# A four-layer graph network on one Trainium2 core: more edge columns fetched row by row by SyncE and ScalarE

## The chip, the cores and the metric

One core of one Trainium2 chip runs the whole program. The metric is the device time of one execution in microseconds. The kernel is a single launch; it has no collectives.

## The reference

Four graph layers follow one another on 12500 nodes with 64 features and 412500 edges sorted by `dst`. Each layer normalises the nodes, gathers or sums along the edges, and adds its result to `x`.

```python
h = jnp.maximum(_layernorm(x), 0.0)
m = h[src] * e                                            # layer 0: weighted sum over dst
x = x + segment_sum(m, dst) @ W.T + b
seg_sum, seg_max, cnt = ... of edge_attr by src           # layer 1: pooling of edge features by src
x = x + relu(concat([seg_sum, seg_max, seg_mean, u]) @ W1 + b1) @ W2 + b2
msg = (h @ Wr)[etype, src] / deg[dst]                     # layer 2: relation-wise sum over dst
x = x + ...
a = softmax over dst of leaky_relu(el[src] + er[dst])     # layer 3: attention over dst
x = x + elu(segment_sum(h[src] * a, dst))
```

## The kernel before

The edges are laid out as 128 partitions by 3224 columns, and the columns are cut into 54 chunks of 60 (the last has 44). A "column" is one edge per partition, 128 edges; fetching a column means fetching 128 rows of a table by index. The program is a sequence of blocks, each closed by a barrier of all engines:

1. a first block normalises the nodes and writes `h_table` to HBM;
2. **wsum0**: chunks 0 to 17 of layer 0. GpSimd gathers a column with one indirect DMA (L559), 60 in a row per chunk, into one of two tiles `lead_rows` (`G`). VectorE multiplies by the weights (L723, which frees the tile: `turned`) and scans along the edges (L759); ScalarE copies the scan to `wsum_S` (L892) and stores it (L894). Beside it VectorE and TensorE count the edges per `src` (L603, L604, L951). Chunk 0 is gathered from the raw `x` and normalised in place by VectorE (L688 to L695), with one square root on ScalarE (L842) in the middle. At the end GpSimd gathers chunk 18 ahead (L206);
3. **the sort**: GpSimd first gathers chunk 19 ahead (L206), then scatters the 33-float edge rows to their place by `src`, again one indirect DMA per column (L1079). VectorE, TensorE and ScalarE compute the places; a chunk is handed over at L1153 (`place_ready`). SyncE loads `sort_lows`, `sort_keys` and `sort_feat` for a chunk as soon as the one before it is handed over (L1032 to L1036). After column 15 of a chunk GpSimd waits that the chunk before has landed, and gives its buffer back (`rows_used`, L1086);
4. **the pooled stage**: chunks 18 to 53 of layer 0, gathered as in wsum0, and beside each of them 90 columns of the sorted rows, which SyncE loads into `pool_row` (L537, L538). ScalarE does per chunk, in this order: the index copy for the gathers two chunks on (L867, `index_ready`), the turn of the sorted rows into `pool_Gf` (L847), the copy to `wsum_S` and its store (L892, L894), and two half copies to `pool_S` with a store each (L856, L858), where the second waits for the first store;
5. the updates, and two more gathered stages, **rel** and **att**, each over all 54 chunks.

In rel and att the last two columns of each full chunk are not gathered by GpSimd. SyncE and ScalarE fetch them row by row: `SingleRows.issue` reads 16 byte addresses at a time into registers (L360, a TENSOR_LOAD) and issues 16 DMAs of one row each (L365). Of the 256 rows of a chunk SyncE takes 160 and ScalarE 96 (`BY_SP`). The addresses are computed once, sent to HBM and read back as one row per chunk (`SingleRows.move`, L344 and L347). Rows of chunk k may be issued when its tile is free, that is, when chunk k-2 has been turned; VectorE reads a chunk when GpSimd's columns, SyncE's rows and ScalarE's rows have all landed (`await_rows`). The table `COLUMNS` says how many columns go this way: none in wsum and in the sort, two in rel and att.

Each engine runs its instructions in program order, so a step that stands behind another on its engine waits for it.

## Time and profile before

| | us |
|---|---|
| median of three runs | 16737.31 |
| lowest and highest | 16735.06 and 16739.51 |
| profiled execution, its own time | 16717.65 |
| its span, first to last instruction | 16715.9 |
| wsum0, from the first gather by index to the barrier | 93 to 1436 |
| sort | 1436 to 5616 |
| pooled stage, up to the fetch of the pooled sums | 5616 to 8195 |

GpSimd is busy for 12576.4 us of the span, in its row of 40 slices at 7 tenths nearly everywhere. An indirect DMA is counted busy for about 0.95 us, and about 0.30 us pass before the next one; the profile calls these "issue", time in which the engine waited for nothing that is shown. So 7 tenths is an engine that never stops. VectorE is at 8 or 9 tenths in wsum0 and the sort, 6 or 7 in the pooled stage and 1 or 2 after that. ScalarE is at 2 tenths or less in most slices, though the time it takes to issue DMAs is not in that figure.

### The profile page before, as it was taken

What the parts mean: (1) busy time and instruction counts of PE and PEld (TensorE: products, weight loads), DVE (VectorE), ACT (ScalarE), POOL (GpSimd) and SP (SyncE); (2) the same over time, 40 slices, a digit from 0 to 9 for tenths busy, and PEclk for the clock granted to TensorE, in tenths of its full rate; (3) what the DMA queues carried; (4) which work ended last, traced back from release to release, by engine and by line L of the source; (5) the groups of instructions that cost most, each with busy time, mean ns of one, the idle gap of its engine ahead of it and who ended that gap; (6) DMA issues with size and microseconds to landing.
All of it is one profiled execution on the core that took longest, in us unless ns stands there. A gap on an engine that the chain in (4) does not pass through costs nothing. (4 is left out here: it accounts for less than half of the span.)

```text
span 16715.9 us, 114264 instructions
## 1 busy us (share of the span) xinstructions
PE 2071.2 (12%) x17217; PEld 1933.7 (12%) x17217; DVE 8380.9 (50%) x5953; ACT 2611.6 (16%) x1261; POOL 12576.4 (75%) x13194
## 2 busy tenths in 40 slices
PE   1212333333333111101320000000000000000000
PEld 1212333333323100101210000000000000000000
DVE  7878988888888677777621111111131222222222
ACT  0000111110101232232221111111110110111101
POOL 7777777777777777777767777777777777777776
PEclk9998666666666555555565555555555555555555
DMA  4222211112121233333532222222233222222222
GB/s 80 55 53 68 71 64 63 68 61 70 61 70 61 89 112 114 108 114 108 103 101 56 56 51 56 56 56 51 56 54 41 57 57 52 57 57 57 52 57 56
DMA packets 686784, 1141.43 MB, mean 68 GB/s; under 512 B 407713, under 2 KB 459500, under 8 KB 644044
## 3 DMA queue, kind: packets, MB, share of 16 engines
q0 software_dynamic: 421952, 380.03, 12.4%
q1 hardware_dynamic: 209740, 325.53, 6.6%
q10 hardware_dynamic: 54336, 428.56, 6.4%
q14 instruction: 620, 5.08, 0.1%
q8 instruction: 136, 2.23, 0.1%
HBM read 613.30 MB, written 519.84 MB: 68 GB/s over the span
## 5 line engine op out<-in xcount | busy, mean ns | idle before, releaser
L1079 POOL DMA_INDIRECT by_src<-H,sort_place_i x3224 | 3122.1, 968 | 983.7 <-issue 983.1
L559 POOL DMA_INDIRECT rel_G<-rel_table,rel_idx x3118 | 2945.7, 945 | 984.6 <-issue 951.3
L559 POOL DMA_INDIRECT att_G<-att_table,att_idx x3118 | 2942.2, 944 | 951.3 <-issue 951.3
L559 POOL DMA_INDIRECT lead_rows<-h_table,wsum_idx x3044 | 2887.2, 948 | 927.7 <-issue 927.7
L753 DVE SCALAR_TENSOR_TENSOR rel_Gf<-rel_Sf,rel_keep_first,rel_Gf 128x64 f32<-128x64 f32 x55 | 18.7, 341 | 3386.3 <-ACT rel_Gf L884 3386.3
L727 DVE TENSOR_TENSOR_SCAN att_near<-att_near,er_in 128x60 f32<-128x60 f32 (+2 forms) x55 | 19.3, 351 | 2835.1 <-issue 1846.7
L1247 PE MATMUL pG<-sort_cnt,sort_lowT 128*128 128x98 f32 x6448 | 1116.0, 348 | 816.7 <-DVE sort_prod L1137 816.7
L1247 PEld LDWEIGHTS pG<-sort_cnt,sort_lowT 128*128 128x128 f32 x6448 | 1071.6, 261 | 824.9 <-DVE sort_prod L1137 824.9
L951 PE MATMUL wsum_C<-wsum_high,wsum_low 128*128 128x98 fp8e4 x6448 | 560.9, 282 | 3369.2 <-DVE wsum_high L604 3369.2
L951 PEld LDWEIGHTS wsum_C<-wsum_high,wsum_low 128*128 128x128 fp8e4 x6448 | 520.1, 142 | 3410.6 <-issue 3410.6
L603 DVE TENSOR_TENSOR wsum_low<-iota_b,wsum_parts 128x3840 fp8e4<-128x3840 bf16 x216 | 891.7, 4128 | 9.8 <-DVE wsum_parts L594 9.8
L1129 DVE TENSOR_REDUCE sort_rank<-sort_keys 128x60 f32<-128x7680 int16 (+1 forms) x54 | 784.8, 14533 | 1.8
L884 ACT COPY rel_Gf<-rel_G 128x3840 f32<-128x3840 f32 (+2 forms) x55 | 358.2, 6513 | 2703.6 <-DMA rel_G<-rel_table,rel_idx 2576.2
L1120 DVE TENSOR_TENSOR sort_lowT<-sort_lows,sort_side 128x7680 f32<-128x7680 uint8 (+1 forms) x54 | 704.6, 13048 | 0.0
L1195 ACT COPY sort_cnt<-pC 128x980 f32<-128x980 f32 x323 | 314.7, 974 | 2486.2 <-PE pC L1239 2455.1
L604 DVE TENSOR_TENSOR wsum_high<-iota_b,wsum_parts 128x2940 fp8e4<-128x2940 bf16 x216 | 689.6, 3193 | 0.0
L1137 DVE TENSOR_TENSOR sort_prod<-pG,sort_high 128x980 f32<-128x980 f32 x323 | 374.3, 1172 | 597.7 <-PE pG L1247 597.6
L856 ACT COPY pool_S<-H 128x2880 f32<-128x2880 f32 (+1 forms) x72 | 363.1, 5043 | 1245.1 <-DVE H L636 1054.4
L892 ACT COPY att_S<-att_Sf 128x3840 f32<-128x3840 f32 (+2 forms) x55 | 397.3, 7223 | 907.4 <-DVE att_Sf L759 907.4
L1498 PE MATMUL att_turn<-ident,att_tail 128*66 128x128 f32 x2 | 0.7, 450 | 4169.2 <-DVE att_tail L818 4169.2
L1239 PE MATMUL pC<-sort_high,sort_low 128*128 128x98 bf16 x3224 | 271.0, 250 | 1943.3 <-DVE sort_lowT L1120 1704.9
L1499 PE MATMUL rel_turn<-ident,rel_tail 128*64 128x128 f32 x2 | 0.7, 446 | 3914.8 <-DVE rel_tail L818 3914.8
(368 smaller groups left out, 7624.2 us busy)
## 6 DMA issues: line engine op xcount, KB each, us to landing
rel_G<-rel_table SPq DMA_DIRECT2D x8480, 0.2 KB
att_G<-att_table SPq DMA_DIRECT2D x8480, 0.3 KB
scan_att<-att_S ACTq DMA_DIRECT2D x53, 1980.0 KB
scan_wsum<-wsum_S ACTq DMA_DIRECT2D x53, 1920.0 KB, 6.5
sort_keys<-key_rows SPq DMA_DIRECT2D x53, 1920.0 KB, 9.6
scan_rel<-rel_S ACTq DMA_DIRECT2D x53, 1920.0 KB
scan_pool<-pool_S ACTq DMA_DIRECT2D x70, 1440.0 KB
rel_G<-rel_table ACTq DMA_DIRECT2D x5088, 0.2 KB
```

The lines of the kernel that those rows point to most:

```text
L559: pool.indirect_dma_start(out=G[s][:, j, :], out_offset=None, in_=table, in_offset=bass.IndirectOffsetOnAxis(ap=idx[s][:, j:j + 1], axis=0 ...
L603: v.tensor_tensor(low[b][:, 0:h, :], iota(P), part(0, P), ALU.is_equal, saturate=False)
L604: v.tensor_tensor(high[b][:, 0:h, :], iota(HT), part(1, HT), ALU.is_equal, saturate=False).then_inc(oh_ready, 1)
L856: nc.scalar.copy(pS[:, 0:w // 2, :].rearrange("p j f -> p f j"), run[:, :, rows]).then_inc(ptaken, 1)
L884: nc.scalar.copy(fresh, G[s][:, 0:w, :].rearrange("p j f -> p f j")).then_inc(turned, 1)
L892: nc.scalar.copy(S[s][:, 0:w, 0:D].rearrange("p j f -> p f j"), run).then_inc(taken_out, 1)
L951: last = mm(C[:, way(w)], low[g % NB][:, j, :], high[g % NB][:, j, :], start=False, stop=False, skip_group_check=True)
L1079: pool.indirect_dma_start(out=by_src, out_offset=bass.IndirectOffsetOnAxis(ap=place_i[s][:, j:j + 1], axis=0), in_=row[s][:, j, :], in_off ...
L1120: v.tensor_tensor(lowT[:, 0:n, :], lows[:, 0:P * n].rearrange("p (x j) -> p j x", j=n), own_near.unsqueeze(2).to_broadcast([P, n, P]), ALU ...
L1129: v.tensor_reduce(rank[:, 0:n], keys[:, 0:P * n].rearrange("p (x j) -> p j x", j=n), AX, ALU.add).then_inc(ranked, 1)
L1137: v.tensor_tensor(by_bank(prod[n % 2][:, 0:m, :]), banked(pG[n % 2], 0, m // wide, wide), by_bank(high[:, at:at + m, :]), ALU.mult).then_i ...
L1247: last = mm(pG[n % 2][:, way(w)], lowT[:, WAYS * g + w, :], cnt[n % 2][:, w, :], start=True, stop=True, skip_group_check=True)
```

## The change

The table `COLUMNS` is raised: two columns a chunk go row by row in the two wsum stages, and one in the sort. In wsum the split is that of rel, 160 rows by SyncE and 96 by ScalarE. In the sort all 128 rows go to SyncE. The address table of wsum is made and moved at the start of wsum0, behind the stores of the key rows. In the sort SyncE sends the places of one column to HBM, reads them back as one row, and issues the 128 row stores, after the loads for the next chunk.

The loads of the sorted rows (`pool_row`) move from SyncE to ScalarE, which issues them between its wait for the pooled scan and the first half copy; at the start of the pooled stage ScalarE also takes over the wait for the last scatters.

```diff
-    COLUMNS = dict(wsum=0, sort=0, rel=2, att=2)
-    BY_SP = dict(wsum=0, rel=160, att=160)
+    COLUMNS = dict(wsum=2, sort=1, rel=2, att=2)
+    BY_SP = dict(wsum=160, sort=128, rel=160, att=160)
...
-                        for k in range(1, c1 + 1):
+                        for k in range(1, c1 + 2):
                             rows_of_chunk(k)
                         sp.wait_ge(rows_stored, 96)
                     if pooled:
...
-                        load_rows(0, 0, SIDE)
-                        for k in range(1, NC):
-                            rows_of_chunk(c0 + k + 1)
-                            load_rows(k // 2, k % 2, SHORT if k == NC - 1 else SIDE)
+                        for k in range(2, NC):
+                            rows_of_chunk(c0 + k)
...
                     if raw:
+                        single.await_moved(act)
+                        act_rows_of_chunk(1)
                         act.wait_ge(raw_var_ready, 1)
                         nc.scalar.activation(raw_root[:], raw_var[:], ACT.Sqrt).then_inc(raw_root_ready, 1)
...
+                    def load_rows(k, w=SIDE):
+
+                        act.wait_ge(pscanned, k + 1)
+                        act.dma_start(prow[:, 0:w, :], sorted_rows(0)[:, k * SIDE:k * SIDE + w, :]).then_inc(prow_loaded, 16)
+                        act.dma_start(prow[:, w:w + 1, :], sorted_rows(1)[:, k * SIDE + w - 1:k * SIDE + w, :]).then_inc(prow_loaded, 16)
...
                         act.wait_ge(pscanned, k + 2)
+                        if k + 1 < NC:
+                            load_rows(k + 1, SHORT if k + 1 == NC - 1 else SIDE)
                         for half in range(2):
...
                         own(i, s)
+                        act_rows_of_chunk(c0 + 2 * i + s + 2)
                         if pooled:
                             take_pooled(2 * i + s)
-                        act_rows_of_chunk(c0 + 2 * i + s + 2)
...
+                    if pooled:
+                        await_scattered()
+                        load_rows(0)
...
+                    if counts and not pooled:
+                        act_rows_of_chunk(c1 + 1)
...
-                        sp.dma_start(single_places[s].unsqueeze(1), place_bytes[s][:], allow_slow_non_contiguous=True).then_inc(places_moved, 16)
+                        sp.dma_start(single_places[s].rearrange("(n p) -> p n", p=P), place_bytes[s], allow_slow_non_contiguous=True).then_inc(places_moved, 16)
                         sp.wait_ge(places_moved, 32 * k + 16)
-                        sp.dma_start(place_row[s][:], single_places[s].unsqueeze(0)).then_inc(places_moved, 16)
+                        sp.dma_start(place_row[s], single_places[s].unsqueeze(0)).then_inc(places_moved, 16)
                         sp.wait_ge(places_moved, 32 * k + 32)
...
+                        issue_rows(sp, k, s, sort_by_sp, scattered_sp_rows)
```

GpSimd's part of the program shrinks by these counts: its indirect DMAs of wsum0, of the two chunks ahead, of the sort and of the pooled stage. Before:

```order
L559 DMA lead_rows<-h_table,wsum_idx 128x64 x1020
L206 DMA lead_rows<-h_table,src_all 128x64 x60
L390 UNCONDITIONAL_BRANCH
L1071 UNCONDITIONAL_BRANCH
L1088 IOTA sort_own_part 128x1
L206 DMA lead_rows<-h_table,src_all 128x64 x60
L1079 DMA by_src<-H,sort_place_i 412674x33 x3224
L978 UNCONDITIONAL_BRANCH
L545 UNCONDITIONAL_BRANCH
L559 DMA lead_rows<-h_table,wsum_idx 128x64 x2024
```

and after, with the line numbers of the changed file:

```order
L547 DMA lead_rows<-h_table,wsum_idx 128x64 x986
L209 DMA lead_rows<-h_table,src_all 128x64 x58
L393 UNCONDITIONAL_BRANCH
L1089 UNCONDITIONAL_BRANCH
L1107 IOTA sort_own_part 128x1
L209 DMA lead_rows<-h_table,src_all 128x64 x58
L1097 DMA by_src<-H,sort_place_i 412674x33 x3171
L992 UNCONDITIONAL_BRANCH
L533 UNCONDITIONAL_BRANCH
L547 DMA lead_rows<-h_table,wsum_idx 128x64 x1958
```

Nothing changes place there; 34, 2, 2, 53 and 66 indirect DMAs are gone.

At the start of wsum0 ScalarE has, before, the square root for chunk 0 as its second instruction of the block:

```order
L839 COPY wsum0_idx1<-src_all 128x60
L842 ACTIVATE raw_root<-raw_var 128x60
L867 COPY wsum0_idx0<-src_all 128x60
L892 COPY wsum0_S<-wsum0_Sf 128x64x60
L894 DMA scan_wsum<-wsum0_S 128x3840
```

After, six pairs of a register load and 16 row DMAs stand between; the last two pairs and what follows:

```order
L363 TENSOR_LOAD wsum_single_ids
L368 DMA lead_rows1<-h_table 1x256 x16
L363 TENSOR_LOAD wsum_single_ids
L368 DMA lead_rows1<-h_table 1x256 x16
L838 ACTIVATE raw_root<-raw_var 128x60
L881 COPY wsum0_idx0<-src_all 128x60
L906 COPY wsum0_S<-wsum0_Sf 128x64x60
L908 DMA scan_wsum<-wsum0_S 128x3840
```

The square root has moved behind the rows of chunk 1, and behind the wait for the address table.

In the pooled stage, one chunk of ScalarE after the change, from the last of its six row pairs to the next chunk's store (before, no row pairs and no `pool_row` loads stood on this engine, the rest in the same order):

```order
L363 TENSOR_LOAD wsum_single_ids
L368 DMA lead_rows<-h_table 1x256 x16
L853 DMA pool_row<-by_src 128x2970
L854 DMA pool_row<-by_src 128x33
L870 COPY pool_S<-H 128x64x45
L872 DMA scan_pool<-pool_S 128x2880
L870 COPY pool_S<-H 128x64x45
L872 DMA scan_pool<-pool_S 128x2880
L881 COPY wsum_idx<-src_all 128x60
L859 COPY pool_Gf<-pool_row 128x2880
L906 COPY wsum_S<-wsum_Sf 128x64x60
L908 DMA scan_wsum<-wsum_S 128x3840
```

The index copy for GpSimd stands behind 96 row DMAs, two loads and two half copies.

## Rows read from the trace of the kernel before

**Rows 1.** The page: busy time of each engine.
```profile
PE 2071.2 (12%) x17217; PEld 1933.7 (12%) x17217; DVE 8380.9 (50%) x5953; ACT 2611.6 (16%) x1261; POOL 12576.4 (75%) x13194
```

**Rows 2.** The page, costliest groups: busy and mean, then idle time before.
```profile
L1079 POOL DMA_INDIRECT by_src<-H,sort_place_i x3224 | 3122.1, 968 | 983.7 <-issue 983.1
```

**Rows 3.** GpSimd's indirect DMAs: ns min/median/max, first and last start in us.
```profile
L1079 POOL DMA_INDIRECT by_src<-H,sort_place_i x3224: 965/969/1012, 1527.0 to 5630.4; - x190
L559 POOL DMA_INDIRECT lead_rows<-h_table,wsum_idx x3044: 940/944/4321, 93.0 to 8162.3; - x191
```

**Rows 4.** Row-by-row issue in rel, the same columns; the third is SyncE's waits.
```profile
L365 SPq DMA_DIRECT2D rel_G<-rel_table x8480: 227/228/1132, 8493.3 to 12267.4; - x198
...
L360 SPq TENSOR_LOAD <-rel_single_ids x530: 1135/1255/3667, 8492.0 to 12260.7; - x177
...
SPq L360 <- ACT rel_Gf L884: 102.2, 33, 5.3
```

**Rows 5.** Timeline of ScalarE in rel: start, duration, engine, line.
```profile
8951.17 0.36 ACTq L894 DMA_DIRECT2D scan_rel<-rel_S  x1
8954.59 41.51 ACTq L365 DMA_DIRECT2D rel_G<-rel_table  x96
```

**Rows 6.** Start of wsum0: DMA share and GB/s last; then timelines.
```profile
107.00:114.00 7.00, 0.00 (x0) 0.00 (x0) 6.93 (x3) 0.00 (x0) 6.09 (x4) 1.00 0.14 16
...
121.45 0.25 ACT L842 ACTIVATE raw_root<-raw_var 128x60 f32<-128x60 f32 x1 [69.62 <-DVE raw_var L692]
...
127.38 6.62 DVE L723 TENSOR_TENSOR wsum_Gf<-lead_rows,wsum_near 128x3840 f32<-128x3840 f32 x1
...
178.63 0.24 ACT L867 COPY wsum_idx<-src_all 128x60 int32<-128x60 int32 x1 [28.91 <-DMA lead_rows<-h_table,wsum_idx]
```

**Rows 7.** SyncE: the address table of att sent out and read back.
```profile
L344 SPq DMA_DIRECT2D single_ids_att<-att_single_own x2: 427/5286/10145, 12404.0 to 12404.4; - x2
L347 SPq DMA_DIRECT2D att_single_ids<-single_ids_att x1: 246/246/246, 12448.1 to 12448.1; - x1
```

**Rows 8.** Timeline from wsum0 to the sort, VectorE and GpSimd.
```profile
1302.22 0.22 DVE L721 COPY wsum_near<-wt_all 128x60 f32<-128x60 f32 x1 [14.03 <-DMA lead_rows<-h_table,wsum_idx]
...
1403.71 6.64 DVE L723 TENSOR_TENSOR wsum_Gf<-lead_rows,wsum_near 128x3840 f32<-128x3840 f32 x1
...
1435.87 0.94 POOL L206 DMA_INDIRECT lead_rows<-h_table,src_all  x1 [0.30 <-POOLq L390]
...
1450.75 2.62 DVE L1158 TENSOR_TENSOR H<-H,streams 128x98 f32<-128x98 f32 x9 [14.63 <-POOL sort_own_part L1088]
...
1526.96 1.01 POOL L1079 DMA_INDIRECT by_src<-H,sort_place_i  x1 [1.47 <-issue]
```

**Rows 9.** Sort: SyncE's third load of a chunk; stretch after it (DMA share, GB/s).
```profile
3073.47 0.43 SPq L1036 DMA_DIRECT2D sort_feat<-in_attr  x1
...
3085.00:3089.00 4.00, 0.00 (x0) 0.00 (x0) 4.00 (x2) 0.00 (x0) 2.91 (x3) 0.50 0.06 13
```

**Rows 10.** Timeline of ScalarE in one chunk of the pooled stage.
```profile
7001.13 6.71 ACT L892 COPY wsum_S<-wsum_Sf 128x3840 f32<-128x3840 f32 x1 [10.52 <-DVE wsum_Sf L759]
...
7043.85 0.33 ACTq L858 DMA_DIRECT2D scan_pool<-pool_S  x1
7049.12 5.05 ACT L856 COPY pool_S<-H 128x2880 f32<-128x2880 f32 x1 [5.30 <-DMA scan_pool<-pool_S]
7054.20 0.33 ACTq L858 DMA_DIRECT2D scan_pool<-pool_S  x1
...
7060.14 5.43 ACT L847 COPY pool_Gf<-pool_row 128x2880 f32<-128x2880 f32 x1
```

**Rows 11.** Timeline at the start of the pooled stage, SyncE and ScalarE.
```profile
5632.60 0.32 SPq L537 DMA_DIRECT2D pool_row<-by_src  x1
...
5639.69 5.34 ACT L847 COPY pool_Gf<-pool_row 128x2880 f32<-128x2880 f32 x1 [22.60 <-DMA pool_row<-by_src]
```

**Rows 12.** GpSimd at the end of the pooled stage.
```profile
8194.58 0.94 POOL L1275 DMA_INDIRECT H<-scan_pool,end_src  x1 [31.31 <-DMA scan_pool<-pool_S]
```

More of the change, by code:

```diff
@@ L412, in gathered_layer @@
                 sp_rows = lead["sp_rows"] if counts else [sem(f"sp_rows{q}") for q in range(TURNS)] if by_sp else []
-                act_rows = [sem(f"act_rows{q}") for q in range(TURNS)] if by_act else []
+                act_rows = lead["act_rows"] if counts else [sem(f"act_rows{q}") for q in range(TURNS)] if by_act else []
                 def await_rows(engine, i, s, w=L):
@@ L895, in own @@
                                           S[s][:, 0:w, :]).then_inc(stored[s], 16)
-                    def act_rows_of_chunk(k):
-                        if by_act and k < FULL:
-                            act.wait_ge(turned, k - c0 + 1)
-                            single.issue(act, k, by_act, G[k % 2][:], table, act_rows)
                     def own_and_pooled(i, s):
@@ L1150, in hand_on @@
                         dve.wait_ge(rows_used, k + 2)
-                        if COLUMNS["sort"] and n == L:
-                            v.tensor_scalar(place_bytes[s][:], place[s][:, L - 1:L], rank[:, L - 1:L], float(4 * (A + 1)), ALU.add, ALU.mult)
+                        if n == L:
+                            for m in range(SC):
+                                j = L - SC + m
+                                v.tensor_scalar(place_bytes[s][:, m:m + 1], place[s][:, j:j + 1], rank[:, j:j + 1], float(4 * (A + 1)), ALU.add, ALU.mult)
                         v.tensor_tensor(place_i[s][:, 0:n], place[s][:, 0:n], rank[:, 0:n], ALU.add).then_inc(place_ready, 1)
```

87 lines of the change are left out of this document (49 added, 38 removed).

## The prediction

> **What bounds the kernel now.** I read the page's busy times first. GpSimd is busy for 75% of the span [rows 1], and behind each of its indirect DMAs stands an idle time of "issue" of 0.305 us (983.7 us over 3224), which no other engine ends [rows 2]. So an indirect DMA costs 0.944 + 0.305 = 1.249 us for a gather and 0.969 + 0.305 = 1.273 us for a scatter. The first and last starts agree: the 3224 scatters run from 1527.0 to 5630.4, 1.273 us each with no gap, and the gathers of the pooled stage run on from there to 8162.3 [rows 3]. GpSimd is the bound from the first gather to the end of layer 0, and a column less saves one such price as long as nothing else becomes late. Then I read the timelines of the engines that take the columns over, and asked in each stage what their turn per chunk would be against GpSimd's: 58 x 1.249 = 72.4 us in wsum, 59 x 1.273 = 75.1 us in the sort. All sums are made against the profiled execution (16717.65 us); the median is 19.7 us above it, and I carry the difference over unchanged.
>
> **The gain.** 34 + 2 + 2 + 66 = 104 gathers by 1.249 is 129.9 us, and 53 scatters by 1.273 is 67.5 us: **197.4 us** if GpSimd never waits. Five waits take from it.
>
> **What a row costs.** The same issue is in the trace of rel. SyncE's 53 x 160 rows take 12267.4 - 8493.3 = 3774 us, of which 102 us are waits: 69.3 us a chunk, 0.43 us a row with its share of the register loads [rows 4]. ScalarE's 96 rows take 41.5 us, and the first comes 3.4 us after the store before it was issued [rows 5]. GpSimd kept its pace of 945 ns there, so I charge its gathers nothing for the extra row DMAs. The register loads are 1.255 us for 16 registers [rows 4]. The Trainium skill (Runtime: NRT & Kernel Launch, Instruction fetch mechanics) says that such a load takes about 200 ns a register even in bulk. By that, 16 would be 3.2 us, and the turns below would be longer by some 10 us; the trace disagrees and is used.
>
> **1. Start of wsum0: 38 us.** Before, the square root came at 121.45, chunk 0 was turned 12.6 us later, at 134.0, and GpSimd started chunk 2 at about 177, without a wait [rows 6]. Now ScalarE first waits for the address table. SyncE sends it out behind the key rows, whose transfers end at about 107 (the DMA share falls to 0.14 there) [rows 6]. The same table took 44 us for att, from the issue at 12404.0 to the read-back at 12448.1 [rows 7]; with 3 us for reading back it is there at about 155. Then come 96 rows, 3 + 41.5 us: the square root is at about 200, chunk 0 turned at 212, GpSimd's chunk 2 starts at 213. With two columns less, GpSimd is ready at 175: it waits 38 us. The next chunks have slack (SyncE's rows of chunk 1 end at 155 + 3 + 69 = 227, chunk 3 is gathered from 286 on).
>
> **2. From wsum0 to the sort: 38 us.** SyncE must issue the rows of chunk 19 before the barrier, and may only when chunk 17 is turned. VectorE starts chunk 16 at 1302.2 and, after two counting passes that nothing here shortens, multiplies chunk 17 from 1403.7 to 1410.4 [rows 8]: 108 us later. Plus 69 us of rows and some 2 us of barrier, the barrier opens 179 us after chunk 16's start. GpSimd has work for 72.4 + 72.4 - 1 = 144 us (chunks 17 and 18). Before, the barrier was hidden altogether: it opened at 1435.8 while GpSimd still had 12 gathers queued [rows 8]. Now GpSimd stands still for 35 us. Then the sort's first chunk: before, GpSimd's first scatter came 91 us after the barrier, 15 of which were VectorE's wait for a small GpSimd instruction behind that queue [rows 8]. The rest, 76 to 77 us, stays, against 72.4 us of gathers for chunk 19: 4 us more, less the 1.2 that were idle before. Together 38.
>
> **3. In the sort: nothing.** SyncE's turn is: three loads until 1.6 us after the hand-over, the place column behind them, since the transfers run until about 12 us after it (the DMA share has fallen to 0.06 by 3085; the third load was issued at 3073.5) [rows 9], 2 us each for the way out and back, 3 us to the first row, and 128 x 0.43 = 55 us: about 73 us, below 75.1. It is close, but GpSimd gets a chunk's places some 40 us before it needs them, so SyncE could be over by 0.8 us on each of 50 chunks without a wait. The cover here is VectorE's chunk of about 67 us, which needs the keys only 28 us after the hand-over.
>
> **4. Start of the pooled stage: 10 us.** ScalarE now waits for the last scatters and issues the first `pool_row` load (5632.6 before, by SyncE) ahead of the index copy that GpSimd needs: 3 us. Then its first turn: `pool_Gf` at +7.1 us [rows 11], the rows of chunk 20, and the two half copies stand before the second index copy. That is 68 us after the copy to `wsum_S` starts and comes 7 us after GpSimd is ready for chunk 21.
>
> **5. The turn of ScalarE in the pooled stage: 41 us.** From one copy to `wsum_S` to the next: 6.7 (copy) + 3.4 + 41.5 (rows) + 0.8 (two `pool_row` loads) + 5.1 (half copy) + 5.3 (until the store has landed) + 5.1 (half copy and issue of its store) + 0.5 (index copy) + 5.4 (`pool_Gf`) = **73.8 us** [rows 5, 10]. Before, the same turn had over 40 us of waits in it. Every part waits only for things that are earlier by then, so the turn is ScalarE's own, and since step 4 leaves it behind GpSimd, each of the 32 chunks from 22 on starts when its index copy lets it. With 73.7 (overlaps of a few tenths) that is 32 x (73.7 - 72.4) = 41 us. The bounds: 72.4, where nothing is lost, and 75, 83 us.
>
> **6. Tail of the pooled stage: 21 us.** The last chunks have no rows, but VectorE's pooled scans have been waiting for `pool_Gf`. Before, GpSimd waited 31.3 us for the last `pool_S` store [rows 12]. Following the chain (index copy of chunk 33, scan, load, half copies, `pool_Gf`, scan, 36 us to the next scan, 17 us to the store) I get 108 us from the index copy, against 56 us of gathers left: 52 us of waiting, 21 more.
>
> Sum: 197.4 - 38 - 38 - 10 - 41 - 21 = **49 us gained**, so 16688 us, and about 16669 for a profiled execution. rel and att are not touched.
>
> **The rivals.**
>
> *All is hidden.* GpSimd stays the only bound: 16540 us. For it speaks that rel and att do just this. Against it, in rel ScalarE has far less to do per chunk, and the two ends of wsum0 are serial. 4%.
>
> *ScalarE's turn fits.* If it is 72.4 or less, steps 5 and 6 and most of the 7 us in 4 go: 197.4 - 38 - 38 - 4 = 117 us gained, 16620. Needed is 1.4 us less than summed. 11%.
>
> *Slower: SyncE's turn in the sort.* If the place column takes 5 us each way and the rows 0.45 us each (57.6 us), the turn is 1.6 + 10.4 + 10 + 3 + 57.6 = 83 us. Past a lead of 40 us, GpSimd then waits 51 x (83 - 75.1) - 40 = 363 us, and the kernel is at 17050. It decides from 75.9 us on, and from 76.9 the whole gain is gone: (76.9 - 75.1) x 51 - 40 = 52. 9%, mostly near that point (16700 to 16850).
>
> *ScalarE's turn is longer.* The wait for the `pool_S` store may grow, since the load of `pool_row`, 1.5 MB, is now in ScalarE's own queue just ahead of it, and 160 + 96 rows are under way. At 75.3 us the gain is nil, at 77 us the kernel is slower by 55 us. 10%.
> The skill's 200 ns a register would be the extreme of this: a turn of about 83 us, 32 x 9.5 = 304 us more, 16990. 1%.
>
> *Issue is not the price.* If the 16 DMA engines were the limit, moving issues would change nothing (16737). Their share is 2 to 4 tenths in this part, but for the key stores. 1%. That is where the Trainium skill (DMA: Bandwidth & Descriptors, Issuing engines are not separate DMA queues) points: it says that starting DMAs from several engines saves only sequencer time, usually small beside the transfer. Here that time is the span itself, so the trace does not bear the rule out as an objection. That the change does not do what it says is excluded by the counts of GpSimd's DMAs in the built program.
>
> **How the numbers follow.** The forecast, steps 1 to 6 with a turn of 73 to 74.6 us, has 64%; its own range is 16660 to 16720 (turn 20 to 70 us lost, start and boundary +-8 each). The range reaches down to the case where the turn fits and up to the first part of the slower ones: 16620 to 16750. About 0.2% (33 us) is what a measurement of this kernel can tell from no change, so faster is below 16704. Of the 64%, 50 lie there and 14 above; with 4 and 11 from the first rivals faster has 65%. Same gets those 14, 5 of the longer turn, 2 of the sort and the 1 of the DMA engines: 22%. Slower has 13%.
>
> **What would show it.** In the profile after: the square root at about 200 instead of 121; GpSimd idle for 35 us at its first gather of the sort's block, waiting for SyncE through the barrier; scatters again 1.273 us apart with no wait; GpSimd waiting for ScalarE's index copy some 30 times, 1 to 2 us each, and copies to `wsum_S` 73 to 74.5 us apart; the last wait of the stage at 52 us. If the scatters show waits for the place computation (`place_ready`), step 3 is wrong; if the pooled chunks stand 72.4 us apart, step 5 is; if the square root is before 165, step 1 is. A different pace of GpSimd's gathers beside rows (not 0.944 us) would make all of it wrong.

## The result and the profile after

| | before | after |
|---|---|---|
| median of 4 runs | 16736.62 us (16735.06 to 16739.51) | 17565.91 us (17564.64 to 17570.26) |
| span of the profiled execution | 16715.9 us | 17568.4 us |

The changed kernel is slower by 829 us: 1.0496 times the kernel before, 95% interval 1.0478 to 1.0514. 16688 was forecast, in a range up to 16750.

The loss is in one stage. GpSimd's indirect DMAs by line (count, ns min/median/max, first and last start), to be held against [rows 3]:

```profile
L1097 POOL DMA_INDIRECT by_src<-H,sort_place_i x3171: 964/970/1009, 1553.6 to 6433.5; - x199
...
L547 POOL DMA_INDIRECT lead_rows<-h_table,wsum_idx x2944: 939/945/4546, 93.2 to 8985.8; - x197
```

A scatter takes 970 ns as before, and there are 53 fewer. Yet they run for 4880 us instead of 4103. At the old pace 3171 of them take 4037 us; 843 us are waiting. The pooled stage, from there to the last gather, takes 2552 us (2532 before). From the list of waits of GpSimd (us in total, times, longest us):

```profile
POOL lead_rows L547 <- ACT wsum_idx L881: 99.5, 33, 7.0
POOL H L1300 <- DMA scan_pool<-pool_S: 51.7, 1, 51.7
POOL lead_rows L547 <- DVE wsum_Gf L711: 36.3, 1, 36.3
POOL sort_own_part L1107 <- POOLq L393: 36.1, 1, 36.1
```

These are steps 4 and 5, step 6, step 1 and step 2 of the forecast. (The 33 waits of the first line hold 0.3 us each that pass before every gather, 10 us in all.) The waits of the sort are not under a name: the page puts them under "issue", and has 1807.6 us of idle time ahead of 3171 scatters, where 0.305 each would be 967:

```profile
L1097 POOL DMA_INDIRECT by_src<-H,sort_place_i x3171 | 3076.0, 970 | 1807.6 <-issue 1799.0
```

What GpSimd waits for is seen on SyncE. One chunk of the sort in its timeline (start, duration, line, what it issues); compare [rows 9]:

```profile
3477.30 0.36 SPq L1062 DMA_DIRECT2D sort_lows<-low_rows  x1
3477.72 0.42 SPq L1063 DMA_DIRECT2D sort_keys<-key_rows  x1
3478.19 0.42 SPq L1066 DMA_DIRECT2D sort_feat<-in_attr  x1
3478.71 0.47 SPq L1072 DMA_DIRECT2D single_places<-H  x1
3495.55 0.24 SPq L1074 DMA_DIRECT2D H<-single_places  x1
3501.47 66.96 SPq L1046 DMA_DIRECT2D by_src<-H  x128
3568.55 0.36 SPq L1062 DMA_DIRECT2D sort_lows<-low_rows  x1
```

SyncE goes round in 91.25 us here, 91.4 in the mean of its turns, and after the first hand-over it waits for no other engine in the sort, only for its own DMAs. GpSimd needs 75.1. At its column 15 GpSimd waits until SyncE's rows of the chunk before have landed, 13.9 us here:

```profile
3478.81 0.97 POOL L1097 DMA_INDIRECT by_src<-H,sort_place_i  x1 [13.92 <-issue]
```

Step 3 had about 73 us for this turn. Of its terms, the rows are off most: 66.96 us for 128, where 55 were forecast. The row DMAs themselves are alike in both places (227 ns, [rows 4]). What differs is the register load ahead of every 16 of them:

```profile
L1041 SPq TENSOR_LOAD <-H x424: 3432/3542/3757, 1574.0 to 6388.7; - x142
...
L363 SPq TENSOR_LOAD <-rel_single_ids x530: 1132/1253/4916, 9334.4 to 13107.0; - x177
...
L363 SPq TENSOR_LOAD <-wsum_single_ids x520: 1136/1255/4673, 154.1 to 8881.0; - x174
```

The median is 3.54 us instead of 1.25, for 16 registers each. Eight of them a chunk make 8 x 2.3 = 18.3 us, and 91.25 - 18.3 = 73.0. So the question for the experiments is why the same instruction costs 2.8 times as much in the sort.

The change put the places into the spare part of `H`. In the built program `H` begins at byte 52448 of its partition, the spare part 19760 bytes further on, and `place_row` 2 words behind that: 72216, which is 8 bytes behind a multiple of 16. The batches of ids begin at multiples of 32 (117408 for rel, 121920 for wsum, 104832 for att, each plus multiples of 64). Theory A is the address. Theory B is something else about the place: the tile was just written by a DMA, or lies in partition 0, or the stage has heavy vector work and 3.8 MB of loads a chunk.

### The profile page after: what moved, and what is told of

It is laid out like the page before. It is cut to its first block and busy times, and to the rows that moved or that the text cites. A ratio compares the mean times of both kernels' runs of the same rounds, so it can differ in the third digit from the quotient of the medians.

```text
span 17568.4 us, 155834 instructions
## 1 busy us (share of the span) xinstructions
PE 1942.9 (11%) x17217; PEld 1813.1 (10%) x17217; DVE 8384.2 (48%) x6008; ACT 2604.8 (15%) x1261; POOL 12454.3 (71%) x13037
## 5 line engine op out<-in xcount | busy, mean ns | idle before, releaser
L1097 POOL DMA_INDIRECT by_src<-H,sort_place_i x3171 | 3076.0, 970 | 1807.6 <-issue 1799.0
L547 POOL DMA_INDIRECT lead_rows<-h_table,wsum_idx x2944 | 2804.6, 953 | 1023.8 <-issue 887.1
L1272 PE MATMUL pG<-sort_cnt,sort_lowT 128*128 128x98 f32 x6448 | 1019.7, 328 | 819.8 <-DVE sort_prod L1156 819.8
L1272 PEld LDWEIGHTS pG<-sort_cnt,sort_lowT 128*128 128x128 f32 x6448 | 975.3, 241 | 827.9 <-DVE sort_prod L1156 827.9
L1264 PEld LDWEIGHTS pC<-sort_high,sort_low 128*128 128x128 bf16 x3224 | 222.9, 116 | 2890.4 <-DVE sort_lowT L1139 2889.3
```

Source lines behind the costliest of these rows:

```text
L547: pool.indirect_dma_start(out=G[s][:, j, :], out_offset=None, in_=table, in_offset=bass.IndirectOffsetOnAxis(ap=idx[s][:, j:j + 1], axis=0 ...
L1097: pool.indirect_dma_start(out=by_src, out_offset=bass.IndirectOffsetOnAxis(ap=place_i[s][:, j:j + 1], axis=0), in_=row[s][:, j, :], in_off ...
L1264: last = mm(pC[:, way(w)], low[:, WAYS * g + w, :], high[:, WAYS * g + w, :], start=False, stop=False, skip_group_check=True)
L1272: last = mm(pG[n % 2][:, way(w)], lowT[:, WAYS * g + w, :], cnt[n % 2][:, w, :], start=True, stop=True, skip_group_check=True)
```

## The experiments

Seven of the fifteen fell on chips where every kernel is much slower, the kernel before too (24142 to 24227 us instead of 16716 to 16737); the section on the hardware has what is different there. Below, these are called slow chips and the others good chips. From the slow chips only durations of single instructions are used, and ratios where it is said. Five of the seven were repeated on a good chip or have a counterpart there; e2_shifted_ids and e14_places_at_16 have not, so what they would cost or gain in time is not known. In the experiments on good chips the kernel before takes 16715 to 16718 us. A ratio is always against the kernel before on the same chip.

### The places at another address (e1_aligned, e5_aligned_again, e7_aligned)

```
-place_row = [spare[0:1, 2 * SC + s * SC * P:2 * SC + (s + 1) * SC * P] for s in range(2)]
+place_row = [spare[0:1, 12 + s * SC * P:12 + (s + 1) * SC * P] for s in range(2)]
```

> The changed kernel with one number changed: `place_row` begins 12 words into the spare part of `H` instead of 2, so that each batch of 16 places that SyncE loads into registers begins at a multiple of 64 bytes of the partition, as the batches of `wsum_single_ids` do (now it begins 24 bytes behind a multiple of 32). Same tile, same partition, same freshness, same stage. Theory A, the address makes the register load slow: the loads of line 1041 fall from 3.43 to 3.76 us to 1.25 us, SyncE's turn from 91.3 us by 8 x 2.3 = 18 us to about 73, GpSimd's scatters stand 1.273 us apart again (75.1 us a chunk), and the kernel is at 17566 - 52 x (91.3 - 75.1) = about 16725 us. Theory B, the load is slow because the tile was just written by a DMA, or because of its partition or the stage: the loads stay at 3.4 to 3.8 us and the time at 17566 us.

> The same kernel as e1_aligned (the changed kernel with `place_row` moved to a multiple of 64 bytes), for a chip on which the kernel before takes 16737 us: where e1_aligned ran, it took 24142 us, since there SyncE and ScalarE often started only one instruction in 1.4 us in the long lists of row DMAs. That run has shown that the loads of the places now take 1.23 us; what it could not show is what this is worth. Theory A: 16725 us, SyncE's turn in the sort about 73 us, scatters 1.273 us apart. If the place column's wait of 16.8 us (16 us behind the loads of the chunk) or anything else in the turn keeps SyncE above 75.1 us, it shows as 52 times the excess.

> The changed kernel with `place_row` at a multiple of 64 bytes, once more, now for the time where the kernel before takes about 16730 us. Theory A (the slow loads are what pushed SyncE's turn over GpSimd's): loads 1.23 us, a turn of about 73 us, scatters 1.273 us apart, 16725 us. If something else in the turn keeps it above 75.1 us, such as the 16.8 us in which the place column goes out behind the loads, the loads are fast and the kernel still stands above that, at 16725 + 52 times the excess.

In e1_aligned (27261 us beside 24142) and e5_aligned_again (27407 beside 24227) the loads took 1.23 us, but the time said nothing on the question. e7_aligned: **16714.17 us beside 16717.61, ratio 0.9999 (0.9989 to 1.0008)**. Moving one tile by 40 bytes takes back all of the 5%. The loads, the scatters, and SyncE's chunk:

```profile
L1041 SPq TENSOR_LOAD <-H x424: 1132/1231/1452, 1572.7 to 5466.3; - x142
```

```profile
L1097 POOL DMA_INDIRECT by_src<-H,sort_place_i x3171: 965/969/1011, 1551.3 to 5588.0; - x199
```

```profile
3454.39 0.36 SPq L1062 DMA_DIRECT2D sort_lows<-low_rows  x1
...
3455.80 0.65 SPq L1072 DMA_DIRECT2D single_places<-H  x1
3472.57 0.24 SPq L1074 DMA_DIRECT2D H<-single_places  x1
3475.76 51.21 SPq L1046 DMA_DIRECT2D by_src<-H  x128
3527.09 0.36 SPq L1062 DMA_DIRECT2D sort_lows<-low_rows  x1
```

This turn is 72.7 us, and the scatters take 4036.7 us, 1.273 each. Tile, partition, stage and freshness are the same, so theory B is out. SyncE's first 28 turns of the sort are 73.2 us each in the mean; after that they are 75.1 us apart, since SyncE has caught up with the hand-over and waits for it.

### The same shift in another stage (e2_shifted_ids)

```
-self.ids = sb(f"{kind}_single_ids", [FULL, self.columns * P], I32, c)
+self.step = BATCH + 1 if kind == "rel" else BATCH
+self.ids = sb(f"{kind}_single_ids", [FULL, self.columns * P // BATCH * self.step], I32, c)
...
-engine.load(registers, self.ids[k:k + 1, r0:r0 + BATCH])
+at = r0 // BATCH * self.step
+engine.load(registers, self.ids[k:k + 1, at:at + BATCH])
```

> The kernel before, with nothing changed but the spacing of the ids of rel in SBUF: a batch of 16 every 17 words instead of every 16, so that the ten loads of SyncE begin 0, 4, 8, 12, 16, 20, 24, 28, 0, 4 bytes behind a multiple of 32 and the six of ScalarE 8, 12, 16, 20, 24, 28. The ids of att keep their spacing, as a control. Theory A: the load costs 1.25 us where it begins at a multiple of 32 bytes and about 3.5 us at 24 behind one, where it does so in the sort of the changed kernel; how it goes between is what this run shows. If all but the multiples of 32 are slow, SyncE's turn in rel is 69.3 + 8 x 2.3 = 88 us against GpSimd's 72.4 and rel is longer by up to 52 x 15 = 800 us (about 17530 us); if multiples of 8 or 16 were fast too it would be less. Theory B: all sixteen loads stay at 1.25 us, since these ids lie long in place, and the time is 16737 us.

24697 us beside 24142, one run on a slow chip, so only the loads count (count, ns min/median/max; att is the control):

```profile
L363 SPq TENSOR_LOAD <-rel_single_ids x530: 275/3526/3907, 10298.1 to 17506.2; - x177
L363 SPq TENSOR_LOAD <-att_single_ids x530: 3/1242/1471, 17865.7 to 24487.6; - x177
```

Batch by batch, medians of the 53 loads of each in us, by the bytes at which the batch begins behind a multiple of 32:

| engine | 0 | 4 | 8 | 12 | 16 | 20 | 24 | 28 |
|---|---|---|---|---|---|---|---|---|
| SyncE | 1.25, 1.26 | 3.63, 3.63 | 3.54 | 1.59 | 0.70 | 3.63 | 3.63 | 3.63 |
| ScalarE | - | - | 7.30 | 0.88 | 1.32 | 3.77 | 3.77 | 3.78 |

Column 12 and SyncE's 16 are disturbed by that chip: the batches of att in the same places of the row are disturbed too (0.70 to 0.80 us). ScalarE's 8 is its first load of each turn, which is slow on good chips too: 3.10 us in att here, and 2.99 and 3.06 us in rel and att of the kernel before on a good chip, all at multiples of 32. That is a second cause of slow loads, and what it is was not asked. What is left is plain: fast at 0 and 16, slow at 4, 8, 20, 24 and 28; 12 stays open.

### Is the step 16 or 32 bytes (e14_places_at_16)

```
-place_row = [spare[0:1, 2 * SC + s * SC * P:2 * SC + (s + 1) * SC * P] for s in range(2)]
+place_row = [spare[0:1, 8 + s * SC * P:8 + (s + 1) * SC * P] for s in range(2)]
```

> The changed kernel with `place_row` 24 bytes further on, at a multiple of 16 bytes that is none of 32. By e2_shifted_ids (ScalarE's batch 16 bytes behind a multiple of 32 took 1.32 us, those 4, 8, 12, 20, 24 and 28 behind mostly 3.5 to 3.8) the step is 16 bytes: loads of 1.23 us and 16714 us, as e7_aligned. Rival, the step is 32 bytes: loads of 3.5 us and about 17560 us, as the changed kernel.

This ran on a slow chip (27395 us beside 24210), but the loads answer:

```profile
L1041 SPq TENSOR_LOAD <-H x424: 2/1228/1425, 2682.9 to 8599.7; - x142
```

The load takes 1.23 us at an address that is a multiple of 16 and not of 32, so a multiple of 16 bytes is enough. The expected 16714 us could not be tested there. Its ratio to the kernel before (1.1315) is that of e5_aligned_again (1.1318), but the kernel with slow loads was not run on such a chip.

### The turn is a sum (e12_places_first)

The slow loads stay, and SyncE sends the place column out and back ahead of the chunk's three loads:

```
 sp.sem_inc(loading, 1)
+if k:
+    send_places(k - 1, 1 - s)      # place_bytes -> single_places -> place_row
 sp.dma_start(lows[:].unsqueeze(1), ...)
```

> The changed kernel with its slow register loads (`place_row` as it is, 8 bytes behind a multiple of 16), but SyncE sends the place column out and back ahead of the three loads of a chunk instead of behind them. This takes the other large part, the wait of 16.8 us, out of SyncE's turn: 91.3 - 16.8 + 2.1 for the way out on free queues = 76.6 us, or 74.5 if the way back is hidden as well by the issues of the loads. Theory (the turn is a sum, and what counts is by how much it exceeds 75.1): 0 to 1.5 us over on each of 52 chunks, 16714 (as e7_aligned) to 16792 us, with the slow loads still at 3.5 us. Rival: the register load is slow in itself and the wait was only filled by it, or the delayed loads of the chunk (2 to 3 us) make VectorE late: above 16850 us.

**17130.48 us beside 16717.57, ratio 1.0247 (1.0232 to 1.0263)**: 338 us above my theory's upper end, and where the rival had put it (above 16850 us). SyncE's chunk shows which number was wrong:

```profile
3467.12 0.36 SPq L1072 DMA_DIRECT2D single_places<-H  x1
3475.56 0.23 SPq L1074 DMA_DIRECT2D H<-single_places  x1
3475.85 0.34 SPq L1064 DMA_DIRECT2D sort_lows<-low_rows  x1
...
3482.02 67.83 SPq L1046 DMA_DIRECT2D by_src<-H  x128
3549.98 0.36 SPq L1072 DMA_DIRECT2D single_places<-H  x1
```

The way out takes 8.4 us with nothing ahead of it, not 2.1; it is 128 transfers of 4 bytes, one a partition. So of the 16.8 us in the changed kernel only half was waiting behind the loads. I had taken this term from the wrong row (the way back, one row of 512 bytes).

Of the rival's two causes, one is out: the loads stay at 3.55 us although the other wait in the turn has halved. The other was that VectorE gets its loads late and is late itself. GpSimd's waits do bear that name now, 402.7 us of them:

```profile
POOL by_src L1103 <- DVE sort_place_i L1180: 402.7, 48, 10.2
```

But VectorE stands idle for 14 us a chunk until its loads come, and SyncE, which issues them, waits for VectorE only once, before the first chunk. The pace is SyncE's turn, 83.1 us in the mean (the one shown has 82.9). The scatters take 4439.3 us, 403 more than 4037. With the rule that is derived below, 53 turns by (83.1 - 75.1) less a cover of 20 us make 404. The turn is a sum, and each us over 75.1 costs 53.

### Each part alone (e3_sort_alone, e9_sort_alone, e4_wsum_alone, e10_wsum_alone)

The kernel before has tiles of their own for the places, at multiples of 64 bytes, so e3 and e9 have fast loads. The edits of e4 and e10 also leave out the place tiles and SyncE's part in the sort.

```
-COLUMNS = dict(wsum=0, sort=0, rel=2, att=2)      # of the kernel before
+COLUMNS = dict(wsum=0, sort=1, rel=2, att=2)      # e3, e9
```

```
-COLUMNS = dict(wsum=2, sort=1, rel=2, att=2)      # of the changed kernel
+COLUMNS = dict(wsum=2, sort=0, rel=2, att=2)      # e4, e10
```

> The kernel before, with the one scattered column a chunk by SyncE in the sort alone (none in wsum), and the places in tiles of their own, whose addresses are multiples of 64. Theory A: SyncE's turn is about 73 us, below GpSimd's 75.1, so each of 53 scatters of 1.273 us is gained: 16737 - 67 = 16670 us, and the register loads take 1.25 us. A rival, that the sort's stage itself (its heavy vector work, 3.8 MB of loads a chunk, 2 queues) makes SyncE slow: a turn near 91 us and about 17510 us.

> The kernel before with the column a chunk by SyncE in the sort alone, the places in tiles of their own at multiples of 64 bytes, once more for the time where the kernel before takes about 16730 us: 53 scatters of 1.273 us less, 67 us below the kernel before.

> The changed kernel without SyncE's scatters in the sort (the place columns are not sent either; all 60 columns by GpSimd): the part of the change in wsum alone, with ScalarE loading the sorted rows. From the two traces: the first scatter is 26.6 us later than before (1553.65 against 1527.0), the sort takes its 4103 us as before, and the pooled stage from the last scatter to the last gather is 2552 against 2532 us: 16737 + 27 + 20 = 16784 us. If instead the pooled stage was slowed by something that the slow sort left behind, it is nearer to the 49 - 67 = 18 us of loss that my forecast gives this part: 16755 us.

> The changed kernel without SyncE's scatters in the sort, once more for the time where the kernel before takes about 16730 us: the first scatter 27 us later and the pooled stage 20 us longer than before, so 47 us above the kernel before. With e9_sort_alone it should add up to e7_aligned: 47 - 67 = 20 us below the kernel before.

Slow chip: e3_sort_alone 24923 us and e4_wsum_alone 26458 us beside 24142. Good chip: **e9_sort_alone 16650.79 us beside 16717.61, ratio 0.9961 (0.9946 to 0.9975)**, 67 us gained, as the 53 scatters had promised. **e10_wsum_alone 16784.18 us, ratio 1.0039 (1.0025 to 1.0053)**, 67 us lost, where I had expected 47: my sum had left out the last wait of GpSimd, which grew by 20 us (51.5 instead of 31.3, [rows 12]). Together they cancel, and e7_aligned, which has both, is within 4 us of the kernel before. So the wsum part of the change was a loss by itself: 104 gathers are worth 130 us, and its waits cost that and 67 more. GpSimd's two largest waits in e10_wsum_alone:

```profile
POOL lead_rows L547 <- ACT wsum_idx L881: 103.7, 34, 7.3
POOL H L1301 <- DMA scan_pool<-pool_S: 51.5, 1, 51.5
```

### ScalarE's wait filled (e8_pool_batch_between)

ScalarE's turn in the pooled stage of the changed kernel, from one copy to `wsum_S` to the next (compare [rows 10]):

```profile
7506.15 6.73 ACT L906 COPY wsum_S<-wsum_Sf 128x3840 f32<-128x3840 f32 x1
...
7515.99 40.72 ACTq L368 DMA_DIRECT2D lead_rows<-h_table  x96
...
7557.78 5.09 ACT L870 COPY pool_S<-H 128x2880 f32<-128x2880 f32 x1 [44.90 <-issue]
...
7569.89 5.05 ACT L870 COPY pool_S<-H 128x2880 f32<-128x2880 f32 x1 [7.02 <-DMA scan_pool<-pool_S]
...
7575.34 0.24 ACT L881 COPY wsum_idx<-src_all 128x60 int32<-128x60 int32 x1 [0.40 <-ACT pool_S L870]
7575.49 5.30 ACT L859 COPY pool_Gf<-pool_row 128x2880 f32<-128x2880 f32 x1
7580.68 6.75 ACT L906 COPY wsum_S<-wsum_Sf 128x3840 f32<-128x3840 f32 x1
```

```
 act.dma_start(scan_pool..., pS[:, 0:w // 2, :]).then_inc(pstored, 16)
+if half == 0 and k < NC - 2:
+    act_rows_of_chunk(c0 + k + 2, -BATCH)      # the last 16 rows, between the half copies
```

> As e7_aligned, and in the pooled stage ScalarE issues the last 16 of its 96 rows of a chunk between the two half copies, where it waited 7.0 us for the `pool_S` store. Theory: ScalarE's turn (75.4 us) is what bounds the pooled stage; it falls to about 68.5, GpSimd's 72.4 is the bound again, 32 x 3.0 = 96 us are won on e7_aligned: about 16630 us. Rival, that the 75.4 us come from elsewhere (the gathers themselves are slower beside the rows, or VectorE is the bound): nothing changes against e7_aligned.

**16645.87 us beside 16717.61, ratio 0.9957 (0.994 to 0.9974)**, 68 us below e7_aligned on the same chip, where 96 were expected. In its list of waits the 104.2 us for ScalarE's index copy have become 7.1, so ScalarE's turn did bound the stage. Of these 97 us, 9 are no gain: they are the 0.3 us that pass before any gather. The last wait grew by 13 (52.0 in e7_aligned), the pooled scans of VectorE and ScalarE ending that much later behind the gathers.

```profile
POOL H L1302 <- DMA scan_pool<-pool_S: 65.1, 1, 65.1
...
POOL lead_rows L547 <- ACT wsum_idx L883: 7.1, 4, 3.3
```

The rest is small: the wait at the start is 39.8 us here and 36.3 in e7_aligned, and the 2944 gathers are busy for 2800.6 us instead of 2796.6. That makes 97 - 9 - 13 - 4 - 4 = 67.

### The start and the boundary (e6_all_mended, e11_start_mended, e13_keys_by_scalar, e15_keys_by_scalar_again)

e6_all_mended is e8_pool_batch_between with the ids sent out first, the square root ahead of ScalarE's first rows, and the rows of chunk 19 issued in the sort (SyncE's at its first chunk, ScalarE's 96 in six batches, one in each of six chunks):

```
+single.move(sp)                                   # ahead of the key stores
 sp.wait_ge(rows_made, 1)
...
-single.await_moved(act)
-act_rows_of_chunk(1)
 act.wait_ge(raw_var_ready, 1)
 nc.scalar.activation(raw_root[:], raw_var[:], ACT.Sqrt).then_inc(raw_root_ready, 1)
+single.await_moved(act)
+act_rows_of_chunk(1)
...
 load_chunk(k, k % 2)                              # SyncE in the sort
+if k == 0:
+    lead_single.issue(sp, lead_chunk, range(0, BY_SP["wsum"]), lead["rows"][1][:], h_table, lead["sp_rows"])
```

> The changed kernel with four edits, each against one of the losses read in its trace. (1) `place_row` at a multiple of 64 bytes, against the slow register loads of the sort. (2) At the start the column of ids is sent out ahead of the key rows, and ScalarE takes the square root before its rows of chunk 1, not behind them. (3) The rows of chunk 19 are issued in the sort (SyncE's 160 in its first chunk, ScalarE's 96 as one batch in each of chunks 2 to 7), not ahead of the barrier. (4) In the pooled stage ScalarE issues its last batch of 16 rows between the two half copies, so that the wait for the first `pool_S` store (7.0 us) has work beside it: its turn is 75.4 - 7 = 68.5 us against GpSimd's 72.4. On a chip where the kernel before takes 16737 us: 16725 (with (1) alone) - 36 - 36 - 32 x 3 = about 16557 us, faster than both. On a chip like that of e1_aligned, where SyncE and ScalarE are the bound for most of the time, the issues cost more than GpSimd's and none of this can win back the 4 in 10 more rows: 27200 us or a little less.

**16620.15 us beside 16717.16, ratio 0.9943 (0.9926 to 0.9959)**, 63 us short of the 16557 that were expected: 28 are what e8_pool_batch_between fell short of its 96, and 36 are the start, where nothing was won. The wait at the boundary is gone. The wait at the start has moved: SyncE sent 40 us of key stores once the ids were back, and only then its rows of chunk 1, for which VectorE waited, and behind it TensorE's counting and GpSimd.

```profile
251.02 0.22 DVE L710 COPY wsum_near<-wt_all 128x60 f32<-128x60 f32 x1 [103.83 <-DMA lead_rows<-h_table]
```

```profile
POOL lead_rows L548 <- PE wsum_C L966: 45.9, 5, 44.6
```

e11_start_mended puts SyncE's rows of chunk 1 ahead of the key stores:

```
 single.move(sp)
+single.await_moved(sp)
+rows_of_chunk(1)
 sp.wait_ge(rows_made, 1)                          # then the six key stores
```

> e6_all_mended with one more edit: at the start SyncE issues its 160 rows of chunk 1 as soon as the ids are read back (126 us there), ahead of the key rows' stores, which nobody reads before the sort. In e6_all_mended SyncE sent the key stores first, its rows of chunk 1 began at 166.7 and VectorE waited for them until 251.0, so that GpSimd waited 44.6 us ahead of chunk 3. Theory: the rows of chunk 1 then run from 129 to 198 us, chunk 1 is turned at about 206, well before GpSimd needs it at 248; the 44.6 us go, and the kernel is at 16620 - 45 = 16575 us, 0.85% below the kernel before. Rival: the key stores behind the rows move the wait to chunk 2's rows or to VectorE, and only part of it comes back.

**16619.08 us beside 16717.57, ratio 0.9941 (0.9927 to 0.9954)**: nothing gained, the rival was right. The wait at the start is 5 us shorter, and the last wait of the stage 11 us longer (72.4 instead of 61.2). The stores now stand ahead of chunk 2's rows, and the wait is 40.1 us ahead of chunk 4:

```profile
123.58 67.44 SPq L368 DMA_DIRECT2D lead_rows<-h_table  x160
...
229.83 120.22 SPq L368 DMA_DIRECT2D lead_rows<-h_table  x234
```

```profile
POOL lead_rows L548 <- PE wsum_C L966: 40.4, 2, 40.1
```

A turn of 69 us against 72.4 wins back 3.4 us a chunk; a lag of 40 us at the start is not caught up for many chunks, wherever in the row it is put. The cause is either SyncE's 39 us or the work of VectorE and TensorE themselves, which GpSimd names. The last kernel takes the stores off SyncE alone:

```
-sp.dma_start(key_rows...)                         # six stores, by SyncE
+if raw and 2 * i + s < 6:
+    store_keys(2 * i + s)                         # one a chunk, by ScalarE behind its rows
```

> e11_start_mended with the six key stores of wsum0 issued by ScalarE, one behind its rows in each of its first six chunks, where it has some 20 us to spare, instead of all by SyncE between its rows of chunks 1 and 2 (191 to 230 us there). Theory: SyncE's 39 us on the key stores are what made the rows of chunk 2 late and GpSimd wait 40.1 us ahead of chunk 4; without them SyncE goes on with chunk 2 at 191, is done at 260, and the wait goes: the first scatter at 1482 instead of 1522 us and the kernel at 16619 - 40 = 16579 us. Rival, VectorE's and TensorE's own work at the start (two counting passes a chunk beside the turning) sets the pace there: the wait stays within 10 us of 40, and so does the time, 16610 to 16620 us.

> The same kernel as e13_keys_by_scalar, for a chip on which the kernel before takes about 16720 us. Theory: SyncE's 39 us on the key stores made the rows of chunk 2 late; the wait of 40 us ahead of chunk 4 goes, the first scatter comes at 1482 instead of 1522 us, 16579 us. Rival, VectorE's and TensorE's own work at the start sets the pace: 16610 to 16620 us. A third case: the wait goes at the start but comes back in the pooled stage's tail, which in e11_start_mended already stood 73 us behind the last gather: first scatter at 1482, and a time above 16579 us by as much as the tail grows.

e13_keys_by_scalar fell on a slow chip (27372 us beside 24210). e15_keys_by_scalar_again: **16577.12 us beside 16715.50, ratio 0.9916 (0.9902 to 0.9929)**. SyncE issues its rows without a break, no wait of GpSimd is left in wsum0 or at the boundary, and the first scatter comes at 1483.8 us:

```profile
123.80 236.38 SPq L368 DMA_DIRECT2D lead_rows<-h_table  x545
```

```profile
L1105 POOL DMA_INDIRECT by_src<-H,sort_place_i x3171: 965/969/1026, 1483.8 to 5520.8; - x199
```

```profile
POOL H L1311 <- DMA scan_pool<-pool_S: 66.1, 1, 66.1
```

It is the fastest version here, 138 us below the kernel before. So the 39 us of stores on SyncE were the cause of the wait at the start, and not VectorE's and TensorE's own work. Of the 197 us that the issues are worth, 59 are missing: 35 are the last wait (66.1 instead of 31.3 [rows 12]), some 12 are gathers that take longer (952 ns in the mean of the 2944 instead of 948), 6 are index waits, and 4 pass at the first scatter. That last wait was left alone.

## Why the prediction was wrong, and where it was right

| step | forecast | measured in the changed kernel |
|---|---|---|
| gain | 197.4 | 67 us for the scatters (e9_sort_alone); the gathers' median held (945 ns), their mean rose from 948 to 953 ns |
| 1, start | 38 | 36.3 |
| 2, boundary | 38 | 36.1, and 2.8 at the first scatter |
| 3, sort | 0 | **843** |
| 4, pooled start | 10 | 3.3 + 7.0 |
| 5, ScalarE's turn | 41 | **93** |
| 6, tail | 21 (a wait of 52) | a wait of 51.7 |

**Step 3 is what failed**, and in it the term "128 x 0.43". The 0.43 us a row was taken from SyncE in rel with its share of the register loads at 1.255 us [rows 4], for rows whose addresses lie at multiples of 32 bytes. In the sort the load costs 3.54 us (e7_aligned shows that it is the address, and e2_shifted_ids shows it in another stage), the rows 0.52 us each, and the turn 91.4 us. Two other terms were off and nearly cancelled: the place column is sent back at 18 us behind the hand-over and not at 14, since its way out takes 8.4 us and not 2 (e12_places_first), and with fast loads 128 rows take 51.2 us and not 55. The step's own terms add up to 74 us (12 + 4 + 3 + 55) where it says about 73. With the loads as I had assumed them the turn is 73.2 us (e7_aligned): near the forecast, but partly by luck, as these errors offset each other.

**The margin, and the lead.** I had written that from 75.9 us on the sort decides and that from 76.9 the whole gain is gone, and gave this side 9%. The side was the right one and the size was not. The 40 us of lead that I subtracted is not there at the start of the sort: SyncE's first turn begins with the hand-over that also lets GpSimd begin.

```profile
1552.88 0.32 SPq L1062 DMA_DIRECT2D sort_lows<-low_rows  x1
```

```profile
1553.65 1.01 POOL L1097 DMA_INDIRECT by_src<-H,sort_place_i  x1 [2.84 <-issue]
...
1739.15 0.97 POOL L1097 DMA_INDIRECT by_src<-H,sort_place_i  x1 [14.79 <-issue]
```

GpSimd asks for SyncE's rows of a chunk 16 scatters into the next one. So SyncE's turns have 16 x 1.273 = 20 us of cover, once for the whole sort. The second turn has used it up: the last line is GpSimd's first wait for the rows. A lead can only grow while SyncE's turn is shorter than 75.1 us, which e7_aligned shows: it gains 1.9 us a chunk there and needs 28 chunks to catch up with the hand-over. With a longer turn none is ever built. The loss is then the number of turns, 53, by the excess, less 20: 53 x (91.4 - 75.1) - 20 = 844, for 843 measured. The forecast's form, 51 x excess - 40, would have given 791 for the same turn. A step forecast at nothing with 2 us of margin and a price of 53 a us needed its largest unproven term bounded; I bounded the way of the places, which mattered less, and took the load's duration over from another tile without asking what it depends on.

**The price of a load.** The Trainium skill (Runtime: NRT & Kernel Launch, Instruction fetch mechanics) has such a load at about 200 ns a register even in bulk. On that page of the Trainium skill such a load reads HBM; here it reads SBUF. I wrote that the trace disagrees, weighed the figure for ScalarE's turn alone and gave it 1%. The runs show both prices: 3.54 / 16 = 0.22 us a register at the sort's address, 1.23 / 16 = 0.08 at a multiple of 16 bytes. By the figure of the Trainium skill the sort's turn would have been an estimated 73 + 8 x 1.95 = 89 us, close to the 91.4 measured. The forecast's "some 10 us" for it was too low as well: 16 us for the eight loads of the sort, 12 for ScalarE's six.

**Step 5**: the form was right (the index copy ends last, some 30 times), the size was not: 3.0 us a chunk instead of 1.3. The 1958 gathers of the pooled stage take 2552 us, where the pace before (2532 us for 2024) gives 2449. Of these 103 us, 10 are step 4's and 93 step 5's: 89 of the 103 are GpSimd's waits for the index copy (99.5 less the 10 of ordinary issue), the others are gathers that take longer. The term is the wait for the first `pool_S` store, 7.0 us where 5.3 was taken from [rows 10]; the turn is 75.4 instead of 73.7. The rival that the turn is longer named this term, and its figure for 75.3 us, a gain of nil, is what e7_aligned measured. e8_pool_batch_between shows that this wait is the price. Why the store lands later (the 1.5 MB load of `pool_row` just ahead of it in the same queue, or the rows under way) was not separated.

**Steps 1, 2, 4 and 6** were right within 3 us each. What they did not say is what comes next: behind ScalarE's late square root stood SyncE's late rows, at nearly the same price (e6_all_mended, e11_start_mended), so that mending the named cause gained nothing until both were gone. One reading had no effect: the share of the DMA engines is 1 or 2 tenths in the sort, not 2 to 4.

The sum, read from the times of the first and last scatter and the last gather: 844 us of miss in the sort, 52 in the pooled stage (103 instead of 51) and 8 behind its last gather, less 2 ahead of the first scatter, make 902, against 17570.26 - 16669 = 901 for the profiled execution.

## What to carry to other kernels

A duration taken over from another place holds only with its operands' address, shape and history; where a step has 2 us of margin a turn and 53 turns, ask that first, and keep what registers are loaded from at multiples of 16 bytes. When one engine takes work from the bound engine in every turn, write its turn as a sum, and count what cover it has at its first turn: a helper slower than the bound engine never builds a lead. After a named wait is taken away, ask which lag stands just behind it; at a start a lag of 40 us stays for a dozen turns when the engine is only 3.4 us a turn faster than the bound.

## What the runs showed of the hardware

- A load of 16 registers from SBUF takes 1.23 to 1.26 us on SyncE (1.32 on ScalarE) in the median if it begins at a multiple of 16 bytes, and 3.5 to 3.6 us (3.8) if it begins elsewhere. The long loads were seen in the sort (24 bytes behind a multiple of 32) and in rel (4, 8, 20, 24 and 28 behind one); 12 behind one stayed open.
- One load escapes this rule: ScalarE's first of a turn takes about 3 us at a multiple of 32 bytes (medians of 53: 2.99 us in rel and 3.06 in att of the kernel before, the five behind it 1.32). In e8_pool_batch_between the sixth of the pooled stage, which now stands behind a half copy and its store, is slow too (median 2.90 us of the 52 loads in both wsum stages, 1.32 in the changed kernel).
- Sending 128 values of 4 bytes, one from each partition, to HBM takes 8.4 us until it has landed when no load stands ahead of it (e12_places_first); SyncE waits 2.1 us in the mean for the 512 bytes to be read back into one partition (110.3 us in the 53 turns of the changed kernel).
- Chips differ. On three of the chips seen, the kernel before took 24142 to 24227 us, on the others 16715 to 16737, with nearly the same gathers (medians of 944 to 947 ns). There, in the lists of row DMAs, SyncE often starts one instruction only every 1.4 us, moves between registers included. The same lines in e7_aligned and in e5_aligned_again (ns min/median/max), first a good chip, then a slow one:

```profile
L368 SPq MOVE rel_G<-rel_table x8480: 29/29/38, 8486.5 to 12259.9; - x198
```

```profile
L368 SPq MOVE rel_G<-rel_table x8480: 1/29/1466, 13506.0 to 20195.1; - x198
```

  The 8480 rows of rel take 3773 us on the one and 6689 on the other. The more rows SyncE and ScalarE issue, the worse: against the kernel before on such a chip, one column in the sort costs 3.2% (1.032, 1.0303 to 1.0337), two in wsum 9.6% (1.0957, 1.0939 to 1.0975), both 12.9% (1.129, 1.1272 to 1.1309), and the version that is 0.8% faster elsewhere is 13.1% slower there (1.1307, 1.1292 to 1.1323). What is different in those chips was not found out.
